# A mixture-of-experts kernel: 39 whole expert tiles, and 38 tiles of which the last two hold two half tiles each

## The reference

```python
xn = _layernorm(x, axis=-1)
x = x + _L0_attn_ref(xn, ...) + _L0_ffn_ref(xn, ...)
...
# _L0_attn_ref: h = causal recurrence of xn @ B_w.T with lam = sigmoid(log_lambda)
y = jnp.einsum('bln,dn->bld', h, C_w) + D * u
...
# _L0_ffn_ref
tcr = jax.nn.one_hot(jnp.argmax(router_probs, axis=-1), E)   # one expert a token
ecr = (ranks < cap)                                          # and only if it ranks below cap
masks = jnp.moveaxis(tcr * ecr, -1, 0)
def body(acc, expert):
    xi = inputs * me[..., None]
    h = jax.nn.gelu(xi @ W1e + b1e, approximate=False)
    return (acc + (h @ W2e + b2e), None)
```

## Time and profile before

| what | value |
|---|---|
| median of 3 runs | 637.82 us (636.33 to 639.37) |
| the profiled execution | 639.68 us |
| its span, first to last instruction | 637.8 us |
| granted clock, mean over the span | 0.943 |
| PE busy | 585.2 us (92%) |
| DVE, ACT, POOL busy | 431.1, 433.0, 460.0 us |
| POOL's indirect DMAs | 78 scatters to out, 78 gathers of base rows |

### The profile page before, as it was taken

One profiled execution on the slowest core, in us unless ns is written; L12 is line 12 of the kernel. 1 busy time (PEld: TensorE's weight loads), 2 busy tenths in 40 slices (PEclk: granted clock), 3 DMA queues, 4 the chain that ended last, 5 costly groups with the idle time before them and its releaser, 6 DMA issues.

```text
span 637.8 us, 16452 instructions
## 1 busy us (share of the span) xinstructions
PE 585.2 (92%) x4597; PEld 496.7 (78%) x4598; DVE 431.1 (68%) x830; ACT 433.0 (68%) x783; POOL 460.0 (72%) x619
## 2 busy tenths in 40 slices
PE   2998868898979999999999999999999999999990
PEld 1565545566869998989898989898898989898880
DVE  5789898788978988875564645555555556455542
ACT  4877678746978977785757576666667575757540
POOL 1999887871055544887878888888888888888466
PEclk9887778877989999999999999999999999999995
DMA  8994776557221315422222211122111211211110
GB/s 309 410 388 136 260 227 180 192 193 264 99 71 32 109 35 160 136 64 67 68 78 77 76 58 58 49 74 72 61 56 53 74 45 55 73 53 34 49 48 13
DMA packets 33587, 72.63 MB, mean 114 GB/s; under 512 B 6519, under 2 KB 19088, under 8 KB 33552
## 3 DMA queue, kind: packets, MB, share of 16 engines
q1 hardware_dynamic: 21488, 46.67, 20.9%
q0 software_dynamic: 11232, 25.20, 13.1%
q10 hardware_dynamic: 832, 0.31, 0.2%
HBM read 50.64 MB, written 27.00 MB: 122 GB/s over the span
## 4 chain that ended last, share of the span: by engine, by line
PE 74%; DVE 10%; ACT 6%; issue 6%; POOL 2%; DMA 1%; ACTq 0%; DVEq 0%; SPq 0%; POOLq 0%
PE ps_bu L888 10%; PE ps_bu L889 10%; PE ps_bu L890 10%; PE ps_t L862 5%; PE ps_t L864 5%; PE ps_t L863 5%; PE ps_y L864 5%; PE ps_y L862 5%; PE ps_y L863 5%; PE ps_y L730 3%; ACT area L532 2%; PE ps_t L698 2%; PE ps_bu L716 2%; PE ps_num L844 1%; POOL out L468 1%
## 5 line engine op out<-in xcount | busy, mean ns | idle before, releaser
L1331 DVE SCALAR_TENSOR_TENSOR ring<-ring,h_scale 128x512 f16<-128x512 f32 x156 | 116.0, 751 | 138.1 <-ACT ring L658 137.3
L888 PE MATMUL ps_bu<-area,ring 128*128 x624 | 170.1, 273 | 0.4 <-issue 0.4
L889 PE MATMUL ps_bu<-area,ring 128*128 x624 | 170.1, 273 | 0.0
L890 PE MATMUL ps_bu<-area,ring 128*128 x624 | 170.1, 273 | 0.0
L658 ACT ACTIVATE ring<-ring,h_act 128x512 f16<-128x512 f32 x144 | 104.0, 722 | 27.1 <-ACT ring L650 27.1
L468 POOL DMA_INDIRECT out<-ring,idx_b x78 | 99.2, 1272 | 18.2 <-issue 13.5
L452 POOL DMA_INDIRECT work<-xn_rows,idx_x x70 | 87.2, 1245 | 24.8 <-issue 24.2
L650 ACT ACTIVATE ring<-ps_t,b1t,inv_in 128x256 f32<-128x256 f32 x156 | 78.5, 555 | 33.2 <-PE ps_t L864 27.9
L478 POOL DMA_INDIRECT work<-base_rows,idx_b x78 | 83.3, 1068 | 18.0 <-issue 16.4
L862 PE MATMUL ps_t<-work,area 128*128 128x256 f16 x312 | 85.1, 273 | 1.7 <-ACT work L560 1.7
L392 POOL TENSOR_TENSOR small<-ones 128x1 f32<-128x1 f32 x152 | 51.0, 335 | 48.5 <-DVE ring L1358 19.5
(11 more groups left out here) (276 smaller groups left out, 1064.8 us busy)
## 6 DMA issues: line engine op xcount, KB each, us to landing
ring<-L_ffn_W SPq DMA_DIRECT2D x14, 1024.0 KB, 6.3
xn_rows<-area SPq DMA_DIRECT2D x8, 1024.0 KB, 8.9
base_rows<-area SPq DMA_DIRECT2D x8, 1024.0 KB, 6.6
area<-L_attn_u SPq DMA_DIRECT2D x7, 1024.0 KB, 18.1
work<-L_ffn_W SPq DMA_DIRECT2D x3, 1024.0 KB, 6.5
area<-L_ffn_W SPq DMA_DIRECT2D x3, 1024.0 KB, 5.6
work<-base_rows,idx_b POOLq DMA_INDIRECT x78
out<-ring,idx_b POOLq DMA_INDIRECT x78
```

What stands on the lines that cost most here:

```text
L888: t.matmul(dst, hh, wh, start=(c == 0), stop=False)
L889: t.matmul(dst, hh, wl, start=False, stop=False)
L890: last = t.matmul(dst, hl, wh, start=False, stop=(c == C - 1))
L1331: v.scalar_tensor_tensor(out=hlo[p][:, cs], in0=h32[:, cs], scalar=h_scale[:, bass.ds(e, 1)], in1=hhi[p][:, cs], op0=ALU.mult, op1=ALU.sub ...
```

## The change

It changes how the slots are cut. Experts 0 to 4 (PAIRED) still get whole tiles of 256 slots and at least one each. Experts 5 to 7 are rounded up to half tiles of 128 only; an odd half goes to one of the last four half slots (LEFT = 72 to 75). NS falls from 78 to 76 and NT from 39 to 38. Tiles 36 and 37 are mixed: each half has its own expert (`half_expert`).

The routing on DVE gets more small operations: constants at b == 13, the parity `odd`, and the place `way` by which the tokens of an odd half are moved. Nine more (`mixed_halves`) stand before DVE's loop. The loops of PE, ACT and DVE run over steps 10 to 35. `up` of a mixed tile has 96 matmuls of 128 columns instead of 48 of 256, and stands interleaved with `down` of the tile before (`mixed`); gelu of such a tile takes sixteen operations of 128 columns instead of eight of 256. The late weights 14 and 15 are both split in step 6. The base rows of tiles 36 and 37 are gathered into `xg` in POOL's steps 38 and 39. The last tile is drained and written by halves.

```diff
-    NT = TOKENS // W + E - 1
-    NS = 2 * NT
+    PAIRED, MIXED = 5, 2
+    NS = TOKENS // P + E + PAIRED - 1
+    NT = NS // 2
+    LEFT = 2 * (NT - MIXED)
...
+        def late_units(j):
+            return {4: (EARLY,), 5: (EARLY + 1,), 6: (EARLY + 2, EARLY + 3)}.get(j, ()) if isinstance(j, int) else ()
...
+            def last_base(j, gate_no):
+                pool.wait_ge(s["f_xt"], j + 1)
+                gate(gate_no)
+                for h in range(2):
+                    g.indirect_dma_start(out=xg[j % 2][:, h * D:(h + 1) * D], out_offset=None, in_=base_dram, ...)
+                return gate_no + 1
...
             for m in range(NT // 4 * 4, NT + 7):
                 gates = step(m, m % 4, gates)
+                if NT <= m < NT + 2:
+                    gates = last_base(m - 2, gates)
...
+            def mixed(j, p):
+                wu = up_weights(j)
+                es = experts_of(pe, j - 1)
+                wd = [pe.snap(e * (2 * UW) + HALF16) for e in es]
+                pe.wait_ge(s["f_xlo"], j + 1)
+                pe.wait_ge(s["f_yr"], j - 2)
+                for n in range(2 * C):
+                    h, i, c = n // C, n % (C // 2), n % C
...
+                    for k in range(K):
+                        t.matmul(dst, wh, xhi[p][:, k, slots], start=(k == 0), stop=False)
+                        t.matmul(dst, wh, xlo[p][:, k, slots], start=False, stop=False)
+                        last = t.matmul(dst, wl, xhi[p][:, k, slots], start=False, stop=(k == K - 1))
...
+                    t.matmul(out_h, hh, wh, start=(c == 0), stop=False)
+                    t.matmul(out_h, hh, wl, start=False, stop=False)
+                    last = t.matmul(out_h, hl, wh, start=False, stop=(c == C - 1))
...
-            with pe.Fori(PEEL // 2, NT // 2) as i:
+            with pe.Fori(PEEL // 2, NT // 2 - 1) as i:
...
-            up(NT - 1, 0, up_weights(NT - 1))
-            down(NT - 2, 1)
-            down(NT - 1, 0)
+            rows_t(NT - 1, 1, NT // 2 - 1)
+            mixed(NT - 2, 0)
+            mixed(NT - 1, 1)
+            down(NT - 1, 1)
...
+            v.tensor_scalar(ends_e, t_incl, float(W), None, ALU.mult)
+            link(v.tensor_scalar(left, t_incl[:, E - 1:E], 2.0, float(LEFT), ALU.mult, ALU.max))
+            link(v.tensor_tensor_scan(half_at, ones[:, 0:E], odd, left, ALU.mult, ALU.add))
+            link(v.tensor_tensor(half_at, half_at, odd, ALU.subtract))
+            link(v.scalar_tensor_tensor(out=way, in0=half_at, scalar=float(P), in1=ends_e, op0=ALU.mult, op1=ALU.subtract))
...
+            for e in range(PAIRED, E):
+                last = v.tensor_scalar(gap[:, e * T:(e + 1) * T], pos4[:, e * T:(e + 1) * T], ends_e[:, e:e + 1],
+                                       way[:, e:e + 1], ALU.is_ge, ALU.mult)
+            link(last)
+            link(v.tensor_tensor(pos4[:, PAIRED * T:TE], pos4[:, PAIRED * T:TE], gap[:, PAIRED * T:TE], ALU.add))
...
+            dve.wait_ge(s["f_o"], NT - 2)
+            dve.wait_ge(gl[1], 32)
+            dve.wait_ge(sc[1], (NT // 2 - 1) * 32)
+            for h, hs_ in enumerate(halves):
+                if h == 0:
+                    dve.wait_ge(s["f_half"], 1)
+                else:
+                    dve.wait_ge(s["f_y"], NT)
```

225 lines of the change are left out of this document (171 added, 54 removed).

## The result

The changed kernel takes 633.24 us (median of 5 runs, 632.77 to 635.05) where the kernel before takes 638.52 in the same comparison (5 runs, 636.33 to 639.37): ratio 0.9923, interval 0.9901 to 0.9945. That is 5.3 us less, where 10.2 were forecast, and 0.4 us above the end of the range. The direction was right, the size was not. The profiled execution took 634.76 us, its span 633.0.

The account below looks back on a forecast made before the run. PE was taken to bound the loop, DVE and POOL the last 17.2 us. After tile, routing and mixed-tile terms H came 4.9 us earlier; with the end 5.3 shorter, that gave 10.2 less: 627.6 us, range 624.8 to 632.8.

Parts of the forecast that it names:

- One tile less: PE's loop has one step less and PE waits for nobody there, so a whole tile is saved: -10.9 us.
- the end: From H, the start of the last low part of h, to the span's end: 18.6 us, before 23.9, so 5.3 shorter.
- the late weights: ACT's split of weights 15 in step 6: adds 2.0 us to ACT, absorbed by slack, so cost 0.
- rival (b): After H: the last three tiles chain as before (23.9 us), so the end is not shorter: 632.9 us; chance 0.07.
- Two mixed tiles: PE in `mixed`: 128-column matmuls at 57 ns make a tile 10.7 us against 10.46; +0.5 us for both.
- rival (a): Narrow matmuls in the mixed tiles are dear: at 81 ns 632.2 us, chance 0.08; at 109 ns 637.6, chance 0.05.
- Rival (c): PE's register work becomes the bound in `mixed`, making the kernel slower: 638.5 us, or 641.9 at higher prices; chance 0.05.
- The routing: DVE before the first tile: added operations ahead of `places` move all tiles by +1.8 us, bounds 1.4 and 2.5.

## Why the prediction was wrong, point by point

- **One tile less, the end, the late weights: right.** From M to T are 389.26 us in the kernel before and 389.12 in the changed one, so neither the late weights nor `mixed_halves` cost PE anything, as forecast. H to the end was 18.57 for 18.6, which refutes rival (b).
- **Two mixed tiles, +0.5 us: the step that failed.** The price of a matmul was right: the forecast took 57 ns for 128 columns, the runs show 55, and without register instructions the two tiles take 21.2 us (forecast 21.4). So rival (a) is refuted, at the 81 ns of the Trainium skill (TensorE: Matmul & The Clock Gate, Back-to-back issue gap) and at 109. What failed is that this was taken for the bound. Of the 4.8 us, 3.1 are 24 chunks at 0.79 instead of 0.66, and 1.6 the hole at the four reads. With both taken out the kernel measured 0.9839, a gain of 10.3 us (7.9 to 12.6). That this is the forecast's 10.2 to 0.1 us is in part luck, since the routing costs more than forecast in that kernel too.
- **Rival (c) had the mechanism, and the wrong price.** It held that a register instruction costs under 0.108 us, since the loop shows no wait with two of them per three matmuls. That counted 0.037 for each matmul in the same stream. The runs show 0.131 for a register instruction and nothing for the matmuls beside it: two make 0.26 in the loop's 0.327, hidden, six make 0.79 in the mixed tile's 0.66. Its 0.93 a chunk was therefore too dear, and its slowdown did not come; on the other side its 0.36 for a read, which stands in no row, was too cheap, against 0.62 to 0.65 in the runs. The rival deserved far more than 0.05, as the one resource whose use per microsecond the change raised by half, with no row that showed how near its limit was.
- **The routing, +1.8 us: mis-sized.** It measured 3.1 to 3.3 by the profiles and 4.5 (3.1 to 5.9) by the times. Its operations take 2.5 and not 1.96: the three of 64 columns and the one of 192 take 1.18 from 163.37 to 164.55 (forecast 0.79), the five small ones 1.16 from 161.48 (forecast 0.95). The 1.4 on top is the collision with POOL: the forecast asked what waits for DVE, not what DVE would now run beside. Some 0.6 comes back behind it, by the clock. In the profile of after R to M is 4.45 longer than before: 3.8 on DVE, less 0.6 behind it, and 1.3 for tile 0 at the low clock level. A routing that began 2 us earlier covers this, which is why the miss at T seems to be only 0.4.
- **What stays open.** The forecast's 10.2, less 4.8 for the mixed tiles and 1.3 to 1.5 for the rest of the routing, is 3.9 to 4.1; measured were 5.3 (3.5 to 6.3). With the numbers constant it is 8.7 to 8.9 by the same working and 10.3 (7.9 to 12.6) by the ratio, off in the same direction but inside. With the 2.7 that the times give for the rest of the routing it is 2.7 in the changed kernel, outside. The repeats that were to settle it fell on disturbed runs. And there the changed kernel was not faster at all but 1% slower (1.0108, 1.0067 to 1.015), so the gain of 0.8% holds for the undisturbed comparison only.

## What to carry over

When a change makes matmuls narrower, count the instructions on PE between them and not only the matmuls: take register instructions per microsecond of array work before and after. "No wait in the loop" says that the loop's own ratio fits, and nothing of a higher one. A number read inside the stream costs a hole that the profile may put down to another engine; compare the starts of the instructions on both sides, and see whether what is read there can be kept from an earlier use or read where the stream has slack. And when a stage is delayed, look at what the other engines do in the place to which it moves.

## What was not expected of the hardware

- A register instruction on PE takes 0.131 us of its stream (1.049 us for eight, 0.79 for six), more than two narrow matmuls of 55 ns, and the nine matmuls and loads among them add nothing.
- DVE's plane operations of 2048 and 1248 columns grew from 1.23 and 0.80 to 1.59 and 1.87 us beside POOL's work on 128x512, and POOL's from 0.69 and 1.26 to 1.21 and 2.08.
- PE's stream runs ahead of the array and keeps a lead: after eight chunks with slack, eight with six register instructions ran at the array's own 0.66.
- A read of an expert's number (a load and two register instructions) took 0.62 to 0.65 us of PE's stream, more than three such instructions: two of them made a hole of 1.3 us, four one of 1.6 behind eight chunks with slack.
- The same kernel took 638, 651 and 670 us in different comparisons, and the order of two kernels turned with it (0.9923 and 1.0108).
